# Attention layers of a four-part transformer block rewritten: scores computed with keys on the partitions, four heads at a time

## The reference

```python
# 16 heads of 16; H = Hadamard; ln = layer norm without weights
def attend(q, k, v, scale, add):            # per head, softmax over keys
    s = einsum('bhqd,bhkd->bhqk', q, k) * scale + add
    return einsum('bhqk,bhkd->bhqd', softmax(s), v)
# A: cross attention, q = ln(x), k = v = context, add = -1e9 where mask == 0
x = x + attend(ln(x), ctx, ctx, 1/4, mask_add) @ W.T + b
# B: Hadamard, 4-bit rounding of tokens, ternary weights
x = x + (round4(ln(x) @ H)) @ ternary(weight).T
# C: cross attention with projections and a bias per head, query and key; then a feed-forward part
c = ln(x); o = attend(c @ Wq.T, ctx @ Wk.T, ctx @ Wv.T, 1/4, bias)
y = c + o @ Wo.T
y = y + gelu(ln(y)*g1 + be1 @ W1.T + b1) @ W2.T + b2     # 256 -> 1024 -> 256
x = x + ln(y)*g2 + be2
# D: mixture of 8 experts, each takes its best 512 tokens; expert products 256 -> 1024 -> 256
x = x + experts(ln(x))
```

## Time and profile before

| | us |
|---|---|
| median of 3 runs (lowest, highest) | 1192.17 (1177.18, 1197.54) |
| span of the profiled execution, first to last instruction | 1184.8 |
| of it the layers | 917 |
| of it the experts | 268 |

### The profile page before, as it was taken

One profiled execution on the slowest core, in us unless ns is written; L12 is line 12 of the kernel. 1 busy time (PEld: TensorE's weight loads), 2 busy tenths in 40 slices (PEclk: granted clock), 3 DMA queues, 4 the chain that ended last, 5 costly groups with the idle time before them and its releaser, 6 DMA issues. The chain is left out here.

```text
span 1184.8 us, 21611 instructions
## 1 busy us (share of the span) xinstructions
PE 982.9 (83%) x6889; PEld 800.1 (68%) x6889; DVE 709.0 (60%) x2101; ACT 662.4 (56%) x1337; POOL 439.0 (37%) x625
## 2 busy tenths in 40 slices
PE   4897799897998989899888998877964329999996
PEld 3686577676776767777766786665743218889985
DVE  3666478585567758666765885652621755666442
ACT  2565467754675685576558577543531005776663
POOL 3312334151334326133422623322211124777762
PEclk9998579986897899698789989877777558999998
DMA  5900023023003202300320220220000403455542
GB/s 179 304 2 1 10 83 97 2 90 107 0 0 125 70 0 89 107 0 0 125 71 0 89 81 1 81 81 1 19 1 20 139 18 95 124 129 135 144 80 27
DMA packets 70976, 80.75 MB, mean 68 GB/s; under 512 B 3312, under 2 KB 67312, under 8 KB 70896
## 3 DMA queue, kind: packets, MB, share of 16 engines
q1 hardware_dynamic: 64752, 71.43, 18.6%
q0 software_dynamic: 6144, 8.39, 4.0%
HBM read 71.43 MB, written 8.39 MB: 67 GB/s over the span
## 5 line engine op out<-in xcount | busy, mean ns | idle before, releaser
L729 ACT ACTIVATE probs<-neg,neg_max 128x256 f32<-128x256 f32 x512 | 231.9, 504 | 57.4 <-DVE neg_max L592 57.0
L600 DVE TENSOR_TENSOR p_lo<-ps_t,p_hi 128x512 f16<-128x512 f32 x256 | 176.3, 689 | 120.7 <-ACT p_hi L737 119.3
L737 ACT ACTIVATE p_hi<-ps_t 128x512 f16<-128x512 f32 x256 | 150.8, 589 | 136.3 <-PE ps_t L376 135.9
L376 PE MATMUL ps_t<-ident,probs 128*128 128x128 f32 x1024 | 200.3, 327 | 6.2 <-ACT probs L729 5.4
L376 PEld LDWEIGHTS ps_t<-ident,probs 128*128 128x128 f32 x1024 | 128.3, 161 | 47.2 <-issue 13.3
L592 DVE CUSTOM_DVE_ANT_0 neg<-ps_s,bias_t 128x256 f32<-128x256 f32 x256 | 97.7, 419 | 59.3 <-PE ps_s L365 29.9
L925 POOL TENSOR_TENSOR o_sum<-o_raw 128x128 f32<-128x128 f32 x64 | 29.9, 467 | 271.2 <-ACT o_raw L821 271.2
L592 DVE CUSTOM_DVE_ANT_0 neg<-ps_s,mask_add 128x256 f32<-128x256 f32 x224 | 85.5, 419 | 60.9 <-issue 36.4
L347 PE MATMUL ps_m<-part_h,select 32*128 32x256 f32 x256 | 79.1, 369 | 44.1 <-DVE part_l L606 18.2
L347 PEld LDWEIGHTS ps_m<-part_h,select 32*128 32x128 f32 x256 | 49.6, 215 | 60.1 <-issue 37.8
L365 PE MATMUL ps_s<-k_stack_C,q_stack_C 64*128 64x256 f32 x288 | 83.0, 378 | 7.2 <-DVE neg_max L592 5.9
(11 more groups left out here) (244 smaller groups left out, 2337.5 us busy)
## 6 DMA issues: line engine op xcount, KB each, us to landing
bias_t<-in_bias SPq DMA_DIRECT2D x16, 2048.0 KB, 8.4
w1e<-in_w1e SPq DMA_DIRECT2D x8, 1024.0 KB
w2e<-in_w2e SPq DMA_DIRECT2D x8, 1024.0 KB, 6.1
ctxT_A<-in_ctxT SPq DMA_DIRECT2D x8, 256.0 KB, 8.2
mask_int<-in_mask SPq DMA_DIRECT2D x8, 256.0 KB, 7.8
v_raw_A<-in_ctx SPq DMA_DIRECT2D x8, 256.0 KB, 7.9
w<-in_w SPq DMA_DIRECT2D x2, 1024.0 KB, 8.9
ctxT_C<-in_ctxT SPq DMA_DIRECT2D x8, 256.0 KB, 2.7
```

The lines of the kernel that those rows point to most:

```text
L376: ins = nc.tensor.matmul(ps_t[u % 2][:, (i * QT + kb) * P:(i * QT + kb + 1) * P], probs[:, u % 2, i, kb * P:(kb + 1) * P], ident[:, :], st ...
L600: nc.vector.tensor_tensor(p_lo[:, u % 4, :], ps_t[u % 2][:, :], p_hi[:, u % 4, :], ALU.subtract).then_inc(lo_ready, 1)
L729: ins = nc.scalar.activation(probs[:, u % 2, i, :], neg[:, u % 4, i, :], ACT.Exp, bias=neg_max[:, u % 4, i:i + 1], scale=-1.0)
L737: nc.scalar.activation(p_hi[:, u % 4, :], ps_t[u % 2][:, :], ACT.Copy).then_inc(hi_ready, 1)
```

## The change

The layers are written anew, and the loop is gone: every engine's program is written out for 104 *positions* (-16 to 87, eight for one batch in the middle). The unit is now a *quad*: four heads of one batch, all 256 queries. A batch has four quads of A and four of C, numbered w = 0 to 3; w = 2c + par, and the pair c of quads covers eight heads. In the middle, A quads of batch b+1 stand at the even positions and C quads of batch b-1 at the odd ones; the first two batches of A and the last two of C stand in four positions in a row.

Per quad everything is in fp32:

- *Row scores* (queries on the partitions, `row_scores`) serve only to find each query's maximum. C's bias in row order is added by DVE in the same instruction that takes the maximum; A's mask is added on PE by a bf16 product with the identity.
- PE transposes the maxima to a row; DVE adds them into a spare row of the query operand, opposite to a -1 in the key operand, so that the next product subtracts them.
- *Key-first scores* (`key_scores`) come out transposed already; C's transposed bias is added by DVE into `probs`, A's mask by PE; ACT takes the exponential.
- Values and sums of a pair of quads are 32 products with 128 rows and 32 columns, each head at its own 32 output partitions; DVE inverts the sums, 128 x 256, and multiplies.

Each head's operands lie on 32 partitions. A round takes two heads of the next quad's row scores (32-row groups 0, 1) and two of the present quad's key-first scores (groups 2, 3); the second round swaps them. The bias is loaded twice, in row order by SP and transposed by POOL, 1 MB a quad each, two buffers each. Stacks, fp32r parts, probability transposes, high and low parts, value splits and `select` are gone; keys and values of A come from DRAM in their spread form.

Side work is spread over half positions s = 0 to 15 of eight positions (two a position, the first after the first round, the second after the second). For a middle batch PE has: 0 f2 (a quarter), 2 w_a, 3 f2, w_o and transposes, 4 w_v, 5 f2 and transposes, 6 Hadamard, 7 transposes, 8 f1 (a quarter), 9 transposes, 10 ternary product and w_k, 11 f1, 12 f1 and transposes, 13 logits and f1, 14 transposes, 15 w_q and f2. DVE has the layer norms, additions and rounding steps in the same half positions; values of a pair come at positions 0, 3, 4 and 7.

The diff, cut to its core:

```diff
-            engine_seg(eng, seg_a(0), None, False, seg_a(1), start_and_prepare)
...
-            with eng.Fori(1, NB - 2) as b:
-                iteration(b)
+def timetable():
+    grid = {}
+    for b in BATCHES:
+        for w in range(4):
+            grid[8 * (b - 1) + (w if b < 2 else 2 * w)] = Quad(A, b, w)
+            grid[8 * (b + 1) + (1 + w if b > NB - 3 else 1 + 2 * w)] = Quad(C, b, w)
+    return grid
+        def pe_maximum_scores(q, half, j, qt):
+            r = slice(32 * j, 32 * j + 32)
+            return nc.tensor.matmul(row_scores[:, j % 2, qt * SEQ:(qt + 1) * SEQ], queries(q)[r, qt * P:(qt + 1) * P],
+                                    keys(q)[r, :], start=(qt == 0), stop=(q.kind == C and qt == QT - 1))
+        def pe_round(pe, now, then, half):
+            if then is not None:
+                pe_wait_maximum(pe, then, half)   # half 0: max_added of now; half 1: max_taken of half 0
+            if now is not None:
+                pe_wait_scores(pe, now, half)     # max_added of now; exp_done or bias_added of the half before
+            of_then, of_now = (0, 2) if half == 0 else (2, 0)
+            for t in range(QT):
+                if then is not None:
+                    for j in (of_then, of_then + 1):
+                        ins_then = pe_maximum_scores(then, half, j, t)
+                if now is not None:
+                    for j in (of_now, of_now + 1):
+                        ins_now = pe_scores(now, half, j, t)
+            if then is not None and then.kind == A:
+                for n in range(2):
+                    ins_then = nc.tensor.matmul(row_scores[:, n, :], ident_b[:, :], mask_bf[:, then.b % 2, 0, :],
+                                                start=False, stop=True)
...
+        def pe_values(pe, q):
+            for what in ("values", "sums"):
+                col = 0 if what == "values" else SEQ
+                for par in range(2):
+                    for kb in range(QT):
+                        for j in range(4):
+                            f = q.c * P + 32 * j
+                            left = v[:, par, kb, f:f + 32] if what == "values" else ones_op[:, par, :]
+                            ins = nc.tensor.matmul(bank[32 * j:32 * j + 32, col:col + SEQ], left,
+                                                   probs[:, (first, last)[par] % 4, j, kb, :],
+                                                   start=(par == 0 and kb == 0), stop=(par == 1 and kb == 1))
+        def pe_layers(pe):
+            for pos in range(FIRST, LAST):
+                i, k = divmod(pos, 8)
+                now, then, past = quad_of(pos), quad_of(pos + 1), quad_of(pos - 1)
+                if now is not None or then is not None:
+                    pe_round(pe, now, then, 0)
+                if past is not None and past.par == 1:
+                    pe_values(pe, past)
+                pe_side(pe, i, 2 * k)
+                if now is not None or then is not None:
+                    pe_round(pe, now, then, 1)
+                pe_side(pe, i, 2 * k + 1)
+                if then is not None:
+                    pe_maximum_rows(pe, then)      # two transposes, after max_taken of both halves
+        def ve_take_maximum(ve, q, half):
+            if q.kind == A:
+                nc.vector.tensor_reduce(of, row_scores[:, :, :].rearrange("p j (t k) -> p j t k", t=QT), AX_X, ALU.max
+                                        ).then_inc(max_taken, 1)
+                return
+            for j in range(2):
+                for qt in range(QT):
+                    ins = nc.vector.tensor_tensor_reduce(row_scores[...], row_scores[...], bias_q[...],
+                        1.0, -3.0e38, ALU.add, ALU.max, of[:, j, qt:qt + 1])
+        def ve_normalise(ve, q):
+            ve.wait_ge(pv_done, n + 1)
+            nc.vector.reciprocal(sum_inv[:, :], ps_x[q.kind][:, SEQ:2 * SEQ]).then_inc(inv_ready, 1)
+            ve.wait_ge(inv_ready, n + 1)
+            nc.vector.tensor_tensor(attnT[q.kind][:, q.c, :], ps_x[q.kind][:, 0:SEQ], sum_inv[:, :],
+                                    ALU.mult).then_inc(norm_done, 1)
+        def ve_layers(ve):
+            for pos in range(FIRST, LAST):
+                for half in range(2):
+                    if then is not None:
+                        ve_take_maximum(ve, then, half)
+                    if now is not None and now.kind == C:
+                        ve_add_bias(ve, now, half)      # 128 x 1024, key_scores + bias_k -> probs
+                    if half == 0:
+                        ve_side(ve, i, 2 * k)
+                if past is not None and past.par == 1:
+                    ve_normalise(ve, past)
+                if then is not None:
+                    ve_add_maximum(ve, then)            # 128 x 256, row_scores + queries -> queries
+                ve_side(ve, i, 2 * k + 1)
+            nc.scalar.activation(of, key_scores[:, :, :], ACT.Exp)   # A; C: in place in probs
+        def po_load_bias(po, q):
+            if m >= 2:
+                po.wait_ge(bias_added, 2 * (m - 2) + 2)
+            nc.gpsimd.dma_start(bias_k[:, m % 2, :, :, :], a["bias_k"][q.b, q.w]).then_inc(ld[f"bias_k{m % 2}"], 16)
+            if m >= 2:                                  # SP, row order
+                sp.wait_ge(max_taken, 2 * NUMBER[C_ORDER[m - 2]] + 2)
+            sp.dma_start(bias_q[:, m % 2, :, :, :], a["bias_q"][q.b, q.w]).then_inc(ld[f"bias_q{m % 2}"], 16)
```

More of the change, by code:

```diff
@@ L18 @@
 from contextlib import ExitStack
+from collections import namedtuple
 import numpy as np
@@ new lines, in pe_f1, with pe_f2 @@
+        def pe_f1(pe, f, n):
+            bank = ps_m[1] if n % 2 == 0 else ps_x[C]
+            for hc in (2 * n, 2 * n + 1):
+                for c in range(DC):
+                    ins = nc.tensor.matmul(bank[:, (hc % 2) * SEQ:(hc % 2 + 1) * SEQ],
+                                           w_1[:, c, hc * P:(hc + 1) * P], zT[:, c, :],
+                                           start=(c == 0), stop=(c == DC - 1))
+            ins.then_inc(S["f1_out"], 1)
+        def pe_f2(pe, f, quarter):
@@ L717, in ve_o_inverse @@
-        def ve_o_inverse(ve, half, i):
-            ve.wait_ge(o_copied, half + 1)
-            nc.vector.reciprocal(o_inv[:, i, :, :], o_raw[:, i, :, 3 * DK:VW]).then_inc(o_inv_ready, 1)
-        def ac_exp(ac, seg, u):
-            g = seg.base + u
-            ac.wait_ge(neg_ready, g + 1)
-            wait(ac, pt_ready, g - 1)
-            for i in range(2):
-                ins = nc.scalar.activation(probs[:, u % 2, i, :], neg[:, u % 4, i, :], ACT.Exp,
-                                           bias=neg_max[:, u % 4, i:i + 1], scale=-1.0)
-            ins.then_inc(exp_ready, 1)
@@ L980, in walk @@
-        def walk(main, prev, ahead, nxt, unit_first, unit_slot, tail, half_work, side):
-            for s in range(UNITS):
-                if main is not None:
-                    if s == 0 and not ahead:
-                        unit_first(main)
-                    unit_slot(main, s, nxt, prev if s < LAG else None)
-                elif s == 0 and prev is not None:
-                    tail(prev)
-                h = halves(s, main, prev)
-                if h is not None:
-                    half_work(*h)
-                side(s)
@@ L1621, in _ @@
             po_start(po)
[L1622 removed]
+            po_layers(po)
             po.wait_ge(S["stored_x"], 16 * NB)
```

1390 lines of the change are left out of this document (603 added, 787 removed).

## The result

The changed kernel takes 1169.25 us (median of 20 runs, 1161.95 to 1190.09) against 1190.46 for the kernel before (20 runs): ratio 0.9867, 95% interval [0.9837, 0.9896]. The ratio counts only runs in the faster of the chip's two states, so it isn't the quotient of the two medians. The kernel is 1.3% faster, where the forecast had 2.7% and a range around it; the whole interval and the measured median lie inside the likeliest case's own range. A gain of over 2% had been given 0.50; what came, a difference within 2%, had 0.21.

What follows compares the result with a forecast made beforehand. No engine was full; each half position hangs on PE and DVE in turn, 96 us a batch against 104. Start +13, six intervals -50, tail 0 and +4: net -33, span 1152, measured 1160; 8-in-10 range 1055 to 1285.

Steps and rivals of the forecast that it cites:

- likeliest case: Whole kernel: the walk's own estimate, 1160 us measured, own range 1115 to 1210, chance 0.40.
- six intervals: Batch 1's first addition to batch 7's: 80 + 91 + 4 x 96 = 555 us instead of 604.6.
- both rivals that doubted it: Four row groups overlap only in part (1220 us, chance 0.07); column groups of the values take turns (1480, 0.05).
- the clock's term: Middle batch: 1 us added to the walk's sum for PE's lower clock level.
- the walk: Middle batch's eight positions priced in program order: sum 96.6, less 1.6 for DVE overlap, plus 1 for the clock: 96 us.
- slower rival: PE waits at normalisations (positions 0, 3, 4, 7) and drops to the lower clock: 108 a batch, 1250 us, chance 0.22.
- The faster rival: Middle batches: cheap reciprocal and PE at the upper clock level give 86 to 88 a batch, 1090 us, chance 0.26.
- 8 to 14: Start: eight A positions with four mask products a round and nothing beside them take 8 to 14 us each.
- Stalls that name no releaser: Unrolled program coming late to the engines: put at nothing; 1% issue in the expert stage would be 37 us over the layers.
- the serial side work of batch 7, 16: End: batch 7's serial side work between the two groups of four C quads, 16 us of the predicted 115.
- position 64 and the output product, 15: End, up to batch 7's second addition: position 64 and the output product, 15 us of the predicted 115.
- the 84: End: two groups of four C quads at 9 to 12 us each, 84 us of the predicted 115.

Runs made afterwards that it cites:

- e5: The changed kernel with five unread PE products in gaps at normalisations (not position 7) and ahead of the first gelu wait; 1125.95 us, 0.9503 of the kernel before.
- e1: The changed kernel with DVE's addition of the maxima to the queries put ahead of the normalisation; 1110.65 us, 0.9407 of the kernel before.
- e9: e1 with the first gelus behind position 6's first exponential and f1's third quarter behind its second round; 1099.77 us, 0.9308 of the kernel before.

## Why the prediction came out as it did

The prediction was right in its sign and near in size, partly by luck, as errors cancel: the start came out 20 us shorter and the six intervals 19 us longer than put. The span of the profiled execution, 1162.4, is 10 above the predicted 1152 (the median lies 6.9 above that span, where 7.4 was added; the time counted for that same execution is 1164.17, only 1.8 above its span, so the rest is that it was one of the shorter ones):

| step | predicted | measured | difference |
|---|---|---|---|
| start, to batch 1's first addition | 168 | 148.1 | -19.9 |
| six intervals | 555 | 573.8 | +18.8 |
| batch 7's first to second addition | 115 | 130.7 | +15.7 |
| from there to the logits | 45 | 43.6 | -1.4 |
| behind the layers | 268.7 | 266.2 | -2.5 |

**The prices of the instructions held.** The first fence has groups of one middle batch of the changed kernel (count, busy us, mean ns). The second has lines of its timeline: the two halves of a pair's values in four column groups, the first and the last products of a round of eight products on four row groups, and a round that has no present quad, four products (eight passes) on two row groups:

```profile
L536 DVE CUSTOM_DVE_ANT_0 row_scores<-row_scores,bias_q 128x256 f32<-128x256 f32 x32 | 12.6, 456 | 18.7 <-PE row_scores L320 18.7
L529 DVE TENSOR_REDUCE row_max_A<-row_scores 128x4 f32<-128x1024 f32 x8 | 9.8, 1226 | 17.2 <-PE row_scores L355 17.2
L554 DVE TENSOR_TENSOR probs<-key_scores,bias_k 128x1024 f32<-128x1024 f32 x8 | 9.7, 1215 | 0.0
L561 DVE RECIPROCAL sum_inv<-ps_x_A 128x256 f32<-128x256 f32 x2 | 3.5, 1748 | 0.0
```
```profile
439.93 1.93 PE L396 MATMUL ps_x_A<-probs,v_op_A 128*32 128x256 f32 x32
...
441.68 1.91 PE L396 MATMUL ps_x_A<-probs,ones_op 128*32 128x256 f32 x32
...
477.11 0.48 PE L320 MATMUL row_scores<-k_op_c,q_op_C 32*128 32x256 f32 x2 [0.88 <-DVE q_op_A L543]
...
477.87 0.38 PE L337 MATMUL key_scores<-q_op_A,k_op_a 32*128 32x256 f32 x2
...
777.98 1.13 PE L320 MATMUL row_scores<-k_op_c,q_op_C 32*128 32x256 f32 x8
```

A's maxima 1.23 (1.2 predicted), the bias 1.22 (1.2), the inverse of 256 elements 1.75 (2.05, from the slope of 8 to 16), values 3.66 from the first start to the last end (3.7). A round takes 1.14 from the first start to the last end (1.15), as long as the 1.13 of half its products on two groups. So four groups run as one, and both rivals that doubted it have fallen. The 3.07 of the Trainium skill ("TensorE: Matmul & The Clock Gate", Part 3, on measured speedup), by which the prediction estimated a round of 1.4, doesn't hold for these products, at 1.14. Only C's maxima were low: each fused step has a read of 0.14 behind it, four stand 0.38 apart rather than 0.34, 1.6 instead of 1.45. Bias loads landed in 5.3 us, and VectorE never waited for one; loop edges are gone.

**The six intervals: the clock's term was too small, and so were the first two intervals.** "1 us goes back for the clock" stands against 7.2 measured (e5). Without it the batch would be 91.5, below the walk's 95; the rest of the walk was 3.5 too long, spread over the positions, most at 2 (9.4 against 8.0). Position 6 was the worst single one (12.2 against 15.3): the gelus' delay was priced, 2.5, but not what stands behind it at half speed; with the clock held up (e5) it took 12.4. So a batch took 98.7 instead of 96. But that is the smaller part of the 18.8. The last four intervals, which the walk prices, took 390.6 instead of 384; the first two took 12 more than the 80 and 91 put for them, numbers that no row stood behind. Their windows in the changed kernel:

```profile
148.06:233.60 85.54, 63.30 (x628) 37.34 (x628) 52.11 (x126) 22.63 (x30) 11.46 (x14) 0.90 0.36 121
233.60:331.31 97.71, 78.39 (x688) 49.21 (x688) 53.64 (x132) 33.07 (x45) 14.14 (x17) 0.90 0.32 107
```

With the fill the second took 93.3 (e5); no run was made for the first.

**The rivals.** That PE starves at the normalisations was the slower rival, with 55 us of PE on the chain and a quarter of the batch at the lower level. Its mechanism was there (a fifth of the batch; the granted clock of 0.90 stayed above the 0.85 named as its sign). Of its places, the clock fell after the waits of positions 0, 3 and 4, not at 7, and also at position 6, which it hadn't named. Its price of 12 us a batch was too high: 7.2, just under the 8 from which it would decide. The faster rival wanted a cheap inverse and the upper level. The changed kernel has neither (1.75 us, clock 0.90). With the inverse behind the addition e1 comes to batches of 89.5 and 1111 us, and only with the gelus moved as well to 87 and 1100 (e9), near that rival's 86 to 88 and 1090.

**Start and end: both mis-sized.** At the start, positions of A took 7.9 to 11.3 us, the low half of "8 to 14", and the first addition to the queries ended at 27.0; GpSimd's mask took 3.65 (3.9 put). No run tested this stretch. At the end "the serial side work of batch 7, 16" and "position 64 and the output product, 15" failed together. From batch 6's last addition to the queries (744.5) to batch 7's first (784.7) it is 40.2, with one quad, the serial work and position 64 in it (35.7 with the clock held up in e5); from batch 7's last addition to the queries (817.5) to its second addition (852.56) it is 35.0, with one quad and the output product in it. That makes 75.2, where the two terms and two quads of 9 to 12 give 49 to 55. In part it was offset: one of the eight quads counted in the 84 was through its position when the stretch began.

**Stalls that name no releaser** were put at nothing, with a bound of 37 over the layers. In the changed kernel "issue" has 5.0% of the chain over the 896 us of the layers, some 45 us, which is over that bound; two thirds of it lie in pieces under 0.5 us, and the longest is 1.1. The 6% of the page is that of the whole span, with one piece of 11.3 in the experts; it can't be held against the 1% in the earlier trace rows, as that chain begins only at 910. The walk's hops and fills hold some of the 45; how many are more wasn't tried.

## What to carry to other kernels

When an engine has two instructions to issue and another engine waits for one of them, try that one first; it is worth looking for in every hand-written order, and here gave more than the rewrite of all layers (4.6% against 1.3%). A long wait of the matrix engine can cost twice, once for itself and once for the clock after it (7.2 us a batch here), so the price of a gap is to be read from the work behind it too. Taking one wait away shows only what it covered: read which releaser comes next on the other engine before moving the step.

## What the hardware showed that I had not expected

Products that nobody reads made the kernel 3.7% faster than the same kernel without them (0.9503 against 0.9867 of before), and leaving 20 products out left the stretch they lie in at 130.7 us (one run): in the 40 us where most of them stood the granted clock was 0.67 instead of 0.88, and PE was busy 30.3 us instead of 31.0. The inverse of 256 elements takes 1.75 us, 6.8 ns each, over four times an addition of the same size (0.42). Four column groups, of which no earlier row told, ran side by side: 64 passes of 256 columns in 3.66 us.
